# Attention with relative positions on one core: scores of two heads at once, logits banks by key tile

## What is computed

```python
q, k, v = proj(Wq, bq), proj(Wk, bk), proj(Wv, bv)          # of layernorm(x); 16 heads of 16
logits = einsum('bhqd,bhkd->bhqk', q, k) + einsum('bhqd,qkd->bhqk', q, embK[idx])
w = softmax(logits)                                          # idx = clip(k - q, -64, 64) + 64
out = einsum('bhqk,bhkd->bhqd', w, v) + einsum('bhqk,qkd->bhqd', w, embV[idx])
x = x + layernorm(out @ Wo.T + bo)
x = x + layernorm(layernorm(x) @ ternary(W).T * alpha + bias)
```

## Time and profile before

| | |
|---|---|
| median of 3 runs | 2637.41 us (2637.28 to 2637.48) |
| profiled execution, span from first to last instruction | 2629.6 us |
| PE busy | 2474.5 us, 94% |
| DVE busy | 2044.9 us, 78% |
| ACT busy | 1552.6 us, 59% |
| POOL busy | 926.1 us, 35% |
| DMA moved | 408.07 MB, mean 155 GB/s |

### The profile page before, as it was taken

One profiled execution on the slowest core, in us unless ns is written; L12 is line 12 of the kernel. 1 busy time (PEld: TensorE's weight loads), 2 busy tenths in 40 slices (PEclk: granted clock), 3 DMA queues, 4 the chain that ended last, 5 costly groups with the idle time before them and its releaser, 6 DMA issues.

```text
span 2629.6 us, 99990 instructions
## 1 busy us (share of the span) xinstructions
PE 2474.5 (94%) x41858; PEld 1901.8 (72%) x41858; DVE 2044.9 (78%) x5306; ACT 1552.6 (59%) x2993; POOL 926.1 (35%) x2211
## 2 busy tenths in 40 slices
PE   5699999999999999999999999999999999999995
PEld 3377777777777777777777777777777777777774
DVE  5577678876888768876788767987678876887786
ACT  3366666565666556665566665566666565666652
POOL 3002534335332443424434253433434334342014
PEclk9699999999999999999999999999999999999997
DMA  6655664557545565455645566445654556545410
GB/s 167 205 159 152 186 174 130 153 156 201 152 149 153 156 183 157 138 161 171 184 137 156 153 179 185 134 140 161 200 165 131 152 155 195 163 137 169 128 54 30
DMA packets 605183, 408.07 MB, mean 155 GB/s; under 512 B 149563, under 2 KB 604475, under 8 KB 604603
## 3 DMA queue, kind: packets, MB, share of 16 engines
q1 hardware_dynamic: 604730, 401.67, 52.8%
HBM read 205.95 MB, written 194.92 MB: 152 GB/s over the span
## 4 chain that ended last, share of the span: by engine, by line
PE 64%; DVE 23%; issue 6%; ACT 2%; SPq 2%; DMA 1%; POOL 1%; DVEq 0%; ACTq 0%; POOLq 0%
PE oacc L800 15%; PE logitsT L770 14%; PE scores L748 12%; DVE maxes L1047 9%; DVE junk L1044 8%; PE logitsT L775 7%; PE misc L705 4%; PE misc L864 3%; ACT wxr L1251 2%; PE misc L722 2%; DVE stats L922 2%; PE misc L825 2%; PE misc L812 1%; PE misc L732 1%; PE misc L850 1%
## 5 line engine op out<-in xcount | busy, mean ns | idle before, releaser
L770 PE MATMUL logitsT<-qs,ks 98*128 98x128 bf16 (+1 forms) x8192 | 977.5, 220 | 15.9 <-ACT wxr L1251 7.9
L1044 DVE CUSTOM_DVE_ANT_1 junk<-scores,bands 128x512 bf16<-128x512 f32 x988 | 678.2, 686 | 338.8 <-PE scores L748 295.3
L1251 ACT ACTIVATE wxr<-logitsT 128x512 f32<-128x512 f32 x1024 | 587.9, 603 | 453.4 <-PE logitsT L770 356.0
L770 PEld LDWEIGHTS logitsT<-qs,ks 98*128 98x128 bf16 (+1 forms) x8192 | 669.1, 99 | 192.0 <-issue 58.1
L1251 ACT ACTIVATE wy<-logitsT 128x512 f32<-128x512 f32 x1024 | 587.3, 597 | 307.5 <-PE logitsT L770 295.2
L748 PE MATMUL scores<-ks,qs 96*128 96x256 bf16 (+6 forms) x3712 | 686.8, 288 | 83.8 <-DVE maxes L1047 38.4
L1047 DVE TENSOR_REDUCE maxes<-scores 128x1 f32<-128x512 f32 x1024 | 701.3, 685 | 1.5 <-PE scores L748 1.5
L748 PEld LDWEIGHTS scores<-ks,qs 96*128 96x128 bf16 (+1 forms) x3712 | 285.1, 98 | 261.8 <-DVE maxes L1047 133.8
L775 PE MATMUL logitsT<-ident,bands 128*128 128x128 f32 x2048 | 463.3, 278 | 0.0
L1280 POOL TENSOR_SCALAR rs<-rs 128x1 int32<-128x1 int32 (+1 forms) x217 | 47.7, 220 | 897.3 <-DVE rs L927 888.2
L775 PEld LDWEIGHTS logitsT<-ident,bands 128*128 128x128 f32 x2048 | 291.7, 142 | 43.5
(11 more groups left out here) (141 smaller groups left out, 2433.9 us busy)
## 6 DMA issues: line engine op xcount, KB each, us to landing
bs<-praw SPq DMA_DIRECT2D x256, 512.0 KB, 4.3
bands<-bs SPq DMA_DIRECT2D x224, 512.0 KB, 4.6
ks<-kd SPq DMA_DIRECT2D x64, 384.0 KB, 4.4
qs<-qd SPq DMA_DIRECT2D x112, 192.0 KB
bands<-bs SPq DMA_DIRECT2D x128, 128.0 KB, 3.3
qd<-qparts SPq DMA_DIRECT2D x60, 192.0 KB, 2.9
kd<-kparts SPq DMA_DIRECT2D x60, 192.0 KB, 2.6
qd<-qparts SPq DMA_DIRECT2D x60, 128.0 KB, 2.6
```

Source lines behind the costliest of these rows:

```text
L770: mm = e.matmul(lt[:, c * P:(c + 1) * P], kk[0:depth, h, kt * P:(kt + 1) * P], qs[i][0:depth, h, :], start=True, stop=not near, skip_group ...
L1044: e.tensor_tensor_reduce(junk[:], scores[:, 0:512].rearrange("p (a c) -> p a c", a=2), banded, 1.0, LOWEST, ALU.add, ALU.max, mx[:, h, 0:1 ...
L1251: e.activation(dst, src, ACT.Exp).then_inc(exp_ready, 1)
```

## The change

Three things change together.

Scores: `row_max` works on two heads at once. New tiles `mks` and `mqs` hold, for head pair p, 48 rows (blocks 1 to 3: three of the six products; `KPARTS` is set anew so that these are the largest) and the three far rows, for one head from partition 0 and for the other from partition 64. They are loaded by DMA of their own (`load_mk`, `load_mq`). A place computes one half (512 columns) for both heads, piece by piece, first side then second, into two separate banks. There are as many pieces and VectorE passes as before. `SLOT` reorders heads in DRAM so that both heads of a pair belong to the same four.

Logits: a bank is one key tile of four heads, where it was four key tiles of one head; "X" and "Y" are places 0 to 3 and 4 to 7 in order of nearness. The exponentials go to `wl` (left near tile), `wm` (middle one, kept for four steps), `wr` and `wy`.

Order: the places are in a table (`PLACES`), many of them moved a little, `LAG` and `HOLD` too, and `with_banks` delays a whole chain of stages when a bank is late. `dynamic_dma_scratch_size=1024` is set.

```diff
-KPARTS = (1, 0, 2, 0, 1, 0)
+KPARTS = (2, 0, 1, 0, 1, 0)
+MAIN = D
+MROWS = 3 * D
+MDEPTH = MROWS + 3
+SLOT = (0, 1, 4, 5, 2, 3, 6, 7)
+PAIRS = HG // 2
...
-QRING, BRING, VRING = 5, 7, 3
+QRING, BRING, VRING, MRING = 5, 7, 3, 3
...
+ 'step': 7.2,
+ 'half': 3.55,
...
+ 'load_mk': (-41.7, -33.7, -25.7, -17.7),
+ 'load_mq': -21.5,
...
+ 'load_q': -32.7,
+ 'raw': (-28.8, -25.4),
...
+ 'row_max': (-12.49, -11.62, -10.75, -9.88, -9.01, -8.14, -7.1, -6.4),
...
+ 'near': (0.0, 0.4, 0.72, 0.98),
+ 'rest': (1.76, 2.1, 2.5, 2.9),
+ 'value_x': 2.3,
+ 'value_y': 4.1,
...
-        w0 = z + 7.2 * i
-        m0 = w0 - 12.5
+        w0 = z + x_["step"] * i
...
-        for h in range(HG):
-            at(m0 + 0.87 * h, "row_max", s, h)
...
+        for p in range(PAIRS):
+            for half in range(2):
+                at(w0 + x_["row_max"][2 * p + half], "row_max", s, p, half)
...
-        scores = ps("scores", S)
+        scores = [ps(f"scores{i}", 512) for i in range(NSCORE)]
...
+        mks = [sb(f"mks{i}", [P, PAIRS, S], BF16) for i in range(2)]
+        mqs = [sb(f"mqs{i}", [P, PAIRS, P], BF16) for i in range(MRING)]
...
-        wxr = sb("wxr", [P, (QUAD * HG + 4) * WIN])
...
+        wm = sb("wm", [P, QUAD, HG, P])
+        wl = [sb(f"wl{i}", [P, 512]) for i in range(2)]
+        wr = sb("wr", [P, 2, 512])
...
+                elif stage == "load_mk":
+                    m, c = k
+                    b, g = divmod(m, G)
+                    sp.wait_ge(k_out[b % 2][c], 96 * (b // 2 + 1))
+                    if m >= 2:
+                        sp.wait_ge(scored, last_scored((m - 1) * T - 1))
+                    for x in range(2):
+                        e.dma_start(mks[m % 2][HALF * x:HALF * x + MROWS, :, c * CT:(c + 1) * CT],
+                                    kd[b % 2][g, MAIN:MAIN + MROWS, PAIRS * x:PAIRS * x + PAIRS,
+                                              c * CT:(c + 1) * CT]).then_inc(mks_in[m % 2][c], 16)
...
-                    pieces = score_pieces(t)
+                    pieces = [x for x in score_pieces(t) if x[0] // 512 == half]
                     for x, (c, key, length, right) in enumerate(pieces):
                         for chunk in range(key // CT, (key + length - 1) // CT + 1):
-                            pe.wait_ge(ks_in[m_ % 2][chunk], 16 * (m_ // 2 + 1))
-                        pe.wait_ge(row_maxed, 2 * u - 1 if c < 512 else 2 * u)
-                        depth = ROWS if right else SPLIT
-                        mm = e.matmul(scores[:, c:c + length], qs[i][0:depth, h, :], kk[0:depth, h, key:key + length],
-                                      start=True, stop=True, skip_group_check=True)
-                        if x == len(pieces) - 1 or pieces[x + 1][0] // 512 != c // 512:
-                            mm.then_inc(scored, 1)
+                            pe.wait_ge(mks_in[m_ % 2][chunk], 32 * (m_ // 2 + 1))
+                        depth = MDEPTH if right else MROWS
+                        for side in range(2):
+                            pe.wait_ge(row_maxed, u + side - NSCORE + 1)
+                            mm = e.matmul(scores[(u + side) % NSCORE][:, c % 512:c % 512 + length],
+                                          mqs[i][HALF * side:HALF * side + depth, p, :],
+                                          kk[HALF * side:HALF * side + depth, p, key:key + length],
+                                          start=True, stop=True, skip_group_check=True)
+                            if x == len(pieces) - 1:
+                                mm.then_inc(scored, 1)
...
-                    for c, kt in enumerate(tiles):
-                        near = kind == "X" and c < 2
-                        depth = ROWS if is_right(t, kt) else FAR
-                        mm = e.matmul(lt[:, c * P:(c + 1) * P], kk[0:depth, h, kt * P:(kt + 1) * P], qs[i][0:depth, h, :],
-                                      start=True, stop=not near, skip_group_check=True)
+                    for j in range(HB):
+                        mm = e.matmul(lt[:, j * P:(j + 1) * P], kk[0:depth, SLOT[HB * blk + j], kt * P:(kt + 1) * P],
+                                      qs[i][0:depth, SLOT[HB * blk + j], :], start=True, stop=not near, skip_group_check=True)
...
+                    for side in range(2):
+                        dve.wait_ge(scored, u + side + 1)
+                        top = mx[:, PAIRS * side + p, half:half + 1]
+                        sc = scores[(u + side) % NSCORE]
+                        if half:
+                            e.tensor_reduce(top, sc[:], AX.X, ALU.max).then_inc(row_maxed, 1)
+                            continue
+                        dve.wait_ge(band_in[v % BRING], band_loads(v))
+                        dve.wait_ge(row_maxed, u + side)
...
-    nc = bacc.Bacc("TRN2", target_bir_lowering=False, num_devices=1)
+    nc = bacc.Bacc("TRN2", target_bir_lowering=False, num_devices=1, dynamic_dma_scratch_size=1024)
```

More of the change, by code:

```diff
@@ L155, in timetable @@
         for blk in range(2):
-            o = w0 + 3.5 * blk
+            o = w0 + x_["half"] * blk
             for j in range(4):
[L158 to L162, removed]
+                at(o + x_["near"][j], "weights", s, 4 * blk + j, "X")
+                at(o + x_["rest"][j], "weights", s, 4 * blk + j, "Y")
@@ L180, in timetable @@
                 continue
[L181 to L185, removed]
-    return with_banks(slots)
-def with_banks(slots):
[L192 to L195, removed]
+            o = z + x_["tail"] + x_["tail_late_by" if s + 2 * QUAD >= STEPS else "tail_by"] * i
@@ new lines, with chain_of, put_back @@
+CHAIN_OF = {stage: chain for chain, stages in CHAINS.items() for stage in stages}
+def chain_of(stage, k):
+    if stage not in CHAIN_OF:
+        return None
+    if stage == "out_norm":
+        return "relative", k[0] // 2
+    return (CHAIN_OF[stage],) + (k[:1] if stage in ("relative", "relative_sum") else k[:2])
+def with_banks(slots):
+    timed, until, late = [], [-1000.0 - i for i in range(NMISC)], {}
+    held = 0
+    queue = sorted(((slot, i, slot, stage, k) for i, (slot, stage, k) in enumerate(slots)), reverse=True)
+    def put_back(entry):
+        at = len(queue)
+        while at and queue[at - 1] < entry:
+            at -= 1
+        queue.insert(at, entry)
+    while queue:
+        slot, i, planned, stage, k = queue.pop()
+        chain, bank = chain_of(stage, k), None
+        if slot < planned + late.get(chain, 0):
+            put_back((planned + late[chain], i, planned, stage, k))
+            continue
@@ L196, in with_banks @@
         if stage in HOLD:
-            bank = held if stage == "relative" and k[2] else until.index(min(until))
             if stage == "relative" and k[2]:
-                slot += kept
+                bank = held
             else:
-                late, slot = max(0, until[bank] - slot), max(slot, until[bank])
+                bank = until.index(min(until))
+                if until[bank] > slot:
+                    if chain:
+                        late[chain] = until[bank] - planned
+                    put_back((until[bank], i, planned, stage, k))
+                    continue
@@ L488, in q_loads, with mq_loads, last_scored @@
             return 32 * sum(1 if tile_of(x) else 2 for x in range(s % QRING, s + 1, QRING))
+        def mq_loads(s):
+            return 64 * sum(1 if tile_of(x) else 2 for x in range(s % MRING, s + 1, MRING))
+        def last_scored(s):
+            return 2 * n("scored", "row_max", s, PAIRS - 1, 1)
         def band_loads(v):
```

315 lines of the change are left out of this document (208 added, 107 removed).

## The result

The changed kernel takes 2714.8 us (2713.2 to 2717.8) against 2637.4 us on the same chip: ratio 1.030, 95% interval 1.028 to 1.031. It is 3.0% slower. The forecast was 2602 us with a range from 2450 to 2685 us, so the time lies above the range too. The profiled execution has a span of 2713.3 us.

What follows compares the result with a forecast made beforehand. TensorE, busy 94%, was taken to set the pace. Terms -50 (score matmuls, mode changes, hand-over), +10 (late VectorE), +3 (logits banks), +2 (loads) gave -35 us: 2594.6 us span, 2602 us forecast, range 2450 to 2685 us.

Steps and rivals of the forecast that it cites:

- The score matmuls: Score matmuls on TensorE: two sides fully overlap, a place costs 0.22 us instead of 0.44, -225 us; bounds 0 and -225.
- R3: Rival on the score matmuls: the two sides run one after the other, 0 + 152 us, 2790 us; chance 0.06.
- The mode changes: TensorE entering and leaving row-group scores: 1595 more changes at 0.095 us, +152 us; bounds 0 and +152.
- R1: Rival on TensorE's mode: row groups cost no mode change, 2427 to 2495 us, middle given as 2470; chance 0.27.
- The hand-over: Score banks passed between TensorE and VectorE: with score matmuls and mode changes -50 us, plus +10 for VectorE being late.
- a late VectorE: VectorE's next pass on bank 0 starts only after side 0's last piece; +10 us taken, ends 0 and +90.
- (a): Way of summing score matmuls, mode changes and bank waits: nothing waits more, -225 + 152 = -73 us.
- (b): Way of summing by the chain that ended last: scores halved -158, TensorE's 64% of the changes +97, together -61 us.
- (c): Way of summing: all 409 waiting score loads are places that gain nothing, -0.22 x (1024 - 409) + 152 = +17 us.
- The logits banks: Six far banks in a row can stall TensorE before logits while ScalarE works; +3 us taken, bounds 0 and 77.
- The loads: About 700 more DMAs on SyncE's queue hide in its waits, priced 0; later start +2 us taken, up to +6.
- R2: Rival on the hand-over: side 1's load waits on VectorE; 480 waiting places give 2670 us, 700 give 2718; chance 0.20.

Runs made afterwards that it cites:

- half_height: Kernel before with one edit: the contraction of its score matmuls stops at 64 rows, nothing paired; 2732.8 us, ratio 1.038.
- before_half_passes: Kernel before with VectorE's row-maximum passes reading only half of the columns of a bank; 2523.8 us, ratio 0.958.
- after_half_passes: Changed kernel with VectorE's row-maximum passes reading only half of the columns of a bank; 2568.6 us, ratio 0.975.
- single_heads: Changed kernel scoring one head at a time over both banks as before, without the extra loads, keeping its logits banks and places; 2620.5 us, ratio 0.995.
- single_heads_loads: single_heads with the changed kernel's extra key and query loads put back, waited for but read by nothing; 2649.8 us, ratio 1.006.

## Why the prediction was wrong, point by point

**The score matmuls.** Full overlap was right in kind and rival R3 falls: the two sides start 3 to 4 ns apart when both banks are free. The size was off: 163 us of streaming instead of 225, because at 399 of 1024 places side 1 starts late. I had put lost overlap into the hand-over and not into this term.

**The mode changes.** Right, with the number: 1603 more for a forecast of 1595, 152 us for 152. That a change to row groups costs what one to column groups costs was an estimate, and half_height shows it. Rival R1 falls. half_height and the changed kernel show 0.09 to 0.10 us in and out for the 64-row mode, in the timelines and in the medians of the whole run; the 152 us of the table are the count times this. The Trainium skill (TensorEngine Tiling (Array Packing), Key Properties) says that changing the tiling mode, as opposed to the tile, drains TensorE; these runs agree, with about 0.1 us at each change, for row groups too.

**The hand-over.** Here the step failed: -50 us for row tiles, changes and hand-over and +10 us for a late VectorE, -40 us together, where the runs show +47 us (2667.5 to 2714.8). I took (a) -73 and (b) -61 as nearer the truth than (c) +17, because TensorE's idle time on these waits was small. The number of waiting loads rose only from 409 to 443 (274 + 169 in the view of waits), and rule (c) with 443 gives -0.22 x 581 + 152 = +24 us. The row tiles came out at 0 under the alternation (2715.7 to 2714.8) and at +35 us without it (2667.5 to 2702.6), so above (a) and (b) in either order. What (c) leaves out, and my +10 us for a late VectorE was meant to hold, is the alternation: +48 us, measured without any row tile, +12 us with them. VectorE's 339 us of idle time before the band pass, which I read as slack, was time in which it waited for TensorE. One further part was in no term: +18 us for the order of the passes. Its mechanism stays open: between the two kernels waiting before scores goes from 147 to 172 us, which says where and not why.

**The chain as a witness.** Summing along the chain, (b), assumed that shares stay when the work on them shrinks. The runs do not bear it out: between before_half_passes and after_half_passes TensorE saves 44 us net (196 less 152) and waits 85 us more. That is no clean test of the chain, since 28 of the 85 us are the late query load.

**The logits banks.** Waiting before logits rose by 26 us (single_heads against before), more than the +3 taken and well inside the bound of 77. With the places the net is -12 us, so this step erred on the other side.

**The loads.** This step failed too. I priced 700 DMAs at nothing because SyncE's queue waits 700 us and more in total. A sum over the run does not tell the slack at the one point in each sequence where writes, band and query load follow each other. The price was 29 us. In the profiled execution, 36.5 us longer than that of single_heads, 19 are direct waits and 8 the start; the rest, among it the stretches at the lower clock, I did not part. In the changed kernel the first score place starts at 58.6 us instead of 57.2, but the second at 82.7 instead of 77.7: the start costs 5 us, within the +6 bounded, and the +2 taken looked at the first place only.

**The rivals.** R2 gave the right sign and, at its upper end, 2718 us, nearly the measured time. But it needed 700 waiting places, and there are 443 waiting loads; its time is right by luck, by a sum of parts that R2 does not contain. For R1 the recorded middle of 2470 is a slip: between 2427 and 2495 it is 2461. The parts in the order in which they were measured are: logits banks and places -12, loads +29, order of passes +18, alternation +48, row tiles -1, together +82 us; on the result's own chip the difference of the medians is 77 us. In the other order the last two are row tiles +35 and alternation +12. The forecast had +3 for the first, +2 for the loads, nothing for the order of passes and -40 for the last two.

**The range** was too low because the small terms were taken near their lower ends at once: +10 of 90, +2 of 6, 0 for the queue, though a change whose two large terms nearly cancel is decided by exactly these. Of the other signs, TensorE's idle time before the logits was 31.5 us, just over the 30 named, and VectorE was busy 2098 us instead of 2045; no run asks why.

## What to carry to other kernels

Before making tiles of a part of the array, count how often the mode would change and price each at what the trace shows for a change (here 0.1 us): a place that adds two changes must stream well over 0.2 us less to pay. If two tiles share a pair of banks with one reader, finish one bank before the other, or the queue behind the second bank's wait holds the first bank back as well; where the alternation is what lets two tiles run together, weigh the streaming that it gives against the waiting. The slack of a DMA queue is to be read at its tightest moment, not from its total of waits: from the end of a load to the start of what needs it. The price of a part can depend on what else is there, so a ladder of parts holds in its own order only.

## What the runs showed of the hardware

A matmul over 64 rows from partition 0 changes the mode of the array even when it runs alone: 0.09 to 0.10 us on each side (half_height). Two matmuls in the two row halves start 3 to 4 ns apart and take the time of one (0.22 us for 512 columns) when both banks are free. Two kinds of loads that cost 4 and 5.5 us alone cost 29 us together. One stall of 2.6 us is followed by a stretch at 1.2 GHz; in single_heads_loads the lower level was seen after six of the seven stalls (2.0 to 4.8 us), not after the seventh (0.9 us). The mean granted clock is 0.971 in the changed kernel and 0.984 in the kernel before.

A version that beats both kernels came out of the study: single_heads, 2620.5 us, 0.5% under the kernel before on its chip.
